# Relation sums of a graph layer: one more product of 128 columns for each tile of edges, into an unused PSUM bank

## The reference

```python
hx = jnp.einsum('ni,rio->rno', x, weight)       # 8 relations
msg = hx[edge_type, src]
agg = jax.ops.segment_sum(msg, dst, num_segments=num_nodes)
node_repr = agg * ALPHA ** 0.5 + h_bias + (x @ loop_weight) * (1.0 - ALPHA) ** 0.5
```

## Time and profile before

| | us |
|---|---|
| time, median of 3 executions | 5958.03 |
| lowest and highest of them | 5939.9 and 5958.66 |
| the profiled execution, its own time | 5956.54 |
| its span, first to last instruction | 5954.5 |

### The profile page before, as it was taken

How to read it: one execution, slowest core, us unless ns; L and a number is a source line. 1 busy time by engine, 2 the same in 40 slices (tenths; PEclk the granted TensorE clock), 3 DMA queues, 4 the chain that set the end, 5 groups by cost and what they waited for, 6 DMA issues and landing times. The chain is left out here.

```text
span 5954.5 us, 72809 instructions
## 1 busy us (share of the span) xinstructions
PE 4261.1 (72%) x18192; PEld 3031.8 (51%) x18193; DVE 2596.7 (44%) x8576; ACT 1703.5 (29%) x3913; POOL 3354.3 (56%) x3387
## 2 busy tenths in 40 slices
PE   5888877655554455557777777776768889889798
PEld 2455545423333333445555555554346667667566
DVE  7655423433343332433333333336944444444682
ACT  3343430000000000123333333333565534433330
POOL 5777665666676666245555555551456666666221
PEclk9999997766667776568787878887889999999898
DMA  6444442433333333132222222226154444444101
GB/s 218 155 157 155 159 161 84 128 92 93 93 90 91 93 95 96 28 69 41 41 43 42 41 41 41 45 39 197 39 147 141 141 119 122 120 119 120 38 1 44
DMA packets 329593, 562.66 MB, mean 94 GB/s; under 512 B 74513, under 2 KB 230302, under 8 KB 322939
## 3 DMA queue, kind: packets, MB, share of 16 engines
q0 software_dynamic: 140096, 319.55, 20.2%
q1 hardware_dynamic: 189213, 239.87, 12.8%
HBM read 459.66 MB, written 99.50 MB: 94 GB/s over the span
## 5 line engine op out<-in xcount | busy, mean ns | idle before, releaser
L963 POOL DMA_INDIRECT e_ring<-table,erow x1040 | 998.0, 960 | 516.7 <-issue 248.5
L1272 PE MATMUL e_sums<-e_ring,e_onehot 128*128 128x257 f32 x2080 | 776.5, 520 | 624.7 <-issue 312.7
L2286 POOL DMA_INDIRECT t_source<-source_rows,t_index x816 | 772.3, 946 | 709.3 <-DVE t_parts L2369 477.7
L1383 POOL DMA_INDIRECT e_ring<-table,esrc x800 | 796.1, 995 | 423.6 <-issue 207.9
L1272 PEld LDWEIGHTS e_sums<-e_ring,e_onehot 128*128 128x128 f32 x2080 | 491.2, 256 | 895.8 <-issue 535.7
L553 POOL DMA_INDIRECT r_ring<-rows,esrc x528 | 584.6, 1107 | 240.2 <-issue 133.4
L2447 PE MATMUL t_out<-t_w,t_hidden 128*128 128x256 f32 x1600 | 540.9, 474 | 169.1 <-issue 164.4
L1459 PE MATMUL e_total<-e_loads,e_times 128*128 128x256 f32 x2176 | 581.8, 400 | 38.7 <-issue 27.9
L2447 PEld LDWEIGHTS t_out<-t_w,t_hidden 128*128 128x128 f32 x1600 | 365.3, 236 | 305.6 <-issue 250.2
L1459 PEld LDWEIGHTS e_total<-e_loads,e_times 128*128 128x128 f32 x2176 | 417.6, 200 | 129.3 <-issue 55.7
L1470 PE MATMUL e_sums<-e_ring,e_onehot 128*128 128x256 f32 x1600 | 435.0, 394 | 53.7 <-DMA e_ring<-table,esrc 28.7
(11 more groups left out here) (492 smaller groups left out, 6386.5 us busy)
## 6 DMA issues: line engine op xcount, KB each, us to landing
table<-r_stage SPq DMA_DIRECT2D x49, 1024.0 KB
e_loads<-table SPq DMA_DIRECT2D x384, 128.0 KB
t_near<-near_rows SPq DMA_DIRECT2D x102, 256.0 KB
m_outputs<-first_outputs SPq DMA_DIRECT2D x49, 512.0 KB
first_outputs<-t_stage SPq DMA_DIRECT2D x96, 256.0 KB
e_ring<-table,erow POOLq DMA_INDIRECT x1040
t_source<-source_rows,t_index POOLq DMA_INDIRECT x816
e_ring<-table,esrc POOLq DMA_INDIRECT x800
```

The costliest lines, as they stand in the source:

```text
L963: eng.indirect_dma_start(ring[:, t % BODY, 0:D], None, table, bass.IndirectOffsetOnAxis(ap=b.erow[:, EARLY + t:EARLY + t + 1], axis=0)).th ...
L1272: eng.matmul(sums[g % SUMS][:, 0:ACCW], onehot[t % ONEHOTS][:, :], ring[:, t % BODY, :], start=(t % GROUP == 0), stop=(t % GROUP == GROUP ...
L1383: eng.indirect_dma_start(ring[:, t % BODY, :], None, table, bass.IndirectOffsetOnAxis(ap=b.esrc[:, FROM + t:FROM + t + 1], axis=0)).then_i ...
L2286: eng.indirect_dma_start(source[s][:, q, :], None, a.source_rows, bass.IndirectOffsetOnAxis(ap=index[s][:, q:q + 1], axis=0)).then_inc(gat ...
```

## The change

From tile 105 on, TensorE makes one more product ahead of each tile's own: the same stationary one-hot matrix with the first 128 of the slot's columns, into `turning`, started and stopped by itself. Nothing waits for it, it counts no semaphore, and nothing reads its result. It stands behind the same two waits as the tile's own product, so it starts when that one would have started, and the tile's own comes after it.

```diff
+    IDLE = P
...
                 eng.wait_ge(matched, t + 1)
                 eng.wait_ge(gathered[t % BODY], 16 * (t // BODY + 1))
+                if t > PUT(CHUNKS * PUTS):
+                    eng.matmul(turning[:, 0:IDLE], onehot[t % ONEHOTS][:, :], ring[:, t % BODY, 0:IDLE],
+                               start=True, stop=True)
                 eng.matmul(sums[g % SUMS][:, 0:ACCW], onehot[t % ONEHOTS][:, :], ring[:, t % BODY, :],
                            start=(t % GROUP == 0), stop=(t % GROUP == GROUP - 1)).then_inc(summed, 1)
```

## The result

The changed kernel took 5967.0 us (median of 20 runs), the kernel before 5948.6 us in the same set (20 runs): a ratio of 1.0036, interval 1.0023 to 1.0048. The forecast of 5845 us, faster, was wrong in sign; the time lies in the range of rival 1 (5940 to 5976), but its mechanism is another: the clock rose and did not pay for the product, as the experiments show.

What follows compares the result with a forecast made beforehand. GpSimd's gather pace was taken as the stage's floor, with late TensorE counts causing stalls; 935 gathers x (1.433 - 1.31) us gain 115 us, so 5958 - 115 = 5843, rounded to 5845 us; range 5785 to 6000.

Steps and rivals of the forecast that it cites:

- rival 1: Changed stage: late counts stay, the higher clock pays for the product; 5958 us, between 5940 and 5976; chance 0.17.
- 171 us: Gathers from 1064 to 2404 us: time lost to stalls beyond GpSimd's undisturbed pace, the most the change can win.
- its prices: Added product on TensorE: 0.25 us a tile at 2.4 GHz, 0.42 us at 1.2 GHz.
- the disputed term: TensorE's late counts in the stage shrink when it is busier: 1.31 instead of 1.433 us a gather, gaining 115 us.
- Both stretches: Before tile 105 and from 1696 to 1745 us: counts taken as prompt, so bad only where TensorE has little to do.
- the interrupted stretch: 1696 to 1745 us, gathers interrupted by seven bias pieces: counts prompt, TensorE never dry, 1.36 us a gather.
- The clock: TensorE's clock in the changed stage: rises from 0.69 to over 0.85, towards 0.95 to 0.97.
- Rival 3: TensorE in the changed stage: clock does not rise, mean 0.69, bursts grow; +140 us, 6100 us; chance 0.08.
- rival 2: At `add`: counts stay late, clock rises, bursts of eight tiles grow; +93 us, 6050 us; chance 0.17.

Runs made afterwards that it cites:

- before_again: The kernel before, unchanged, traced once more on a chip whose counts come promptly; 5056 us.
- after_again: The changed kernel once more, on the same chip as before_again; 1.0003 times the kernel before.
- set 3: Runs on a prompt chip with TensorE's counts made late through SyncE, among them relay4 and relay4_product; the kernel before took 5063 us there.
- relay4: Kernel before with one count per eight tiles, passed on by SyncE after four small transfers from group 14 on; 5300 us, 1.0469 times before.
- relay4_product: relay4 with the added product of 128 columns; 5415 us, 1.0691 times the kernel before, 115 us more than relay4.
- relay2: relay4 with two transfers instead of four, on a late chip; 6154 us, 1.0249 times the kernel before.
- relay2_product: relay2 with the added product, on a late chip; 6223 us, 1.0368 times the kernel before.
- relay_half: relay4 with its four transfers in every other six groups only, on a late chip; 6098 us, 1.0167 times the kernel before.
- relay_half_product: relay_half with the added product, on a late chip; 6126 us, 1.0203 times the kernel before.
- pause_8: Kernel before with an operation of about 1 us on GpSimd ahead of every eighth gather from the first changed tile on; 1.0174 times before.

## Why the prediction was wrong

**What held.** GpSimd's gather pace is the floor of the stage, and 171 us are what stalls take: on the prompt chips the 1040 gathers span 1317 us instead of 1514, 197 us less. The product does lie between gathers where TensorE follows them (ratios of 1.0000 to 1.0007). 1870 more matmuls ran (18192 to 20062). Of its prices the one at half clock was right and the one at full clock too high: in bursts a tile takes 0.66 us with it and took 0.48 without at the full clock, 1.29 and 0.85 at the half, so 0.18 and 0.44 instead of 0.25 and 0.42.

**The step that failed** is "the disputed term": "the counts are bad just where TensorE has little to do. I take that they shrink". They hardly did: 6.21 us late on average after 6.41, GpSimd idle 467 us instead of the forecast's 337, `add` waiting 872 us instead of well below 843. And the premise is refuted. On the prompt chips TensorE runs the same products in the same loop, at a clock of 0.61, and every count comes at once. The lateness goes with the chip on which the kernel runs.

Both stretches that were to bear the premise out were misread. Before tile 105 the counts were not prompt. GpSimd stood there for them, as the same 106 gathers show, in before from 890 to 1064 us and in before_again from 815 to 948 us:

```profile
L963 POOL DMA_INDIRECT e_ring<-table,erow x106 | 100.7, 950 | 73.7 <-PE e_sums L1272 37.3 <-issue 24.0 <-remote 12.4
```

```profile
L963 POOL DMA_INDIRECT e_ring<-table,erow x106 | 102.1, 964 | 32.3 <-issue 20.7 <-PE e_sums L1272 11.6
```

The first 104 of them came one in 1.65 us on the late chip and one in 1.27 us on the prompt one. `add` waits next to nothing there on either (1.3 and 1.2 us), because VectorE itself comes to it late, so its waits can't tell whether counts are prompt. And the interrupted stretch holds four of the seven bias pieces and not seven; the first three lie before it, and between the first and the second a count is 14.8 us late and VectorE stands for it:

```profile
1666.92 2.01 DVE L1189 TENSOR_TENSOR features<-features,e_bias 128x1792 f32<-128x1792 f32 x1
1683.81 0.48 DVE L1168 SCALAR_TENSOR_TENSOR big<-e_sums,within,big 128x257 f32 x1 [14.00 <-remote]
1685.38 2.02 DVE L1189 TENSOR_TENSOR features<-features,e_bias 128x1792 f32<-128x1792 f32 x1
```

So the pieces do not make counts prompt either. Whether a slower pace of the gathers does is not settled by any run.

**The clock** was forecast over 0.85 and reached 0.77, and TensorE's busy time was 880 us and not about 735. The direction of the clock was right. It stayed under 0.85 in the traces in which TensorE stands again and again, and where TensorE only waits for the next gather (0.98) the time didn't depend on it. Rival 3 is out: the clock rose. The page of the Trainium skill that spoke for it (TensorE: Matmul & The Clock Gate, psum-queue depth-cycling) tells of another kernel, in bf16 with 512 columns. Here the trace doesn't agree with it: in after_again every product changes bank, and the clock is 0.98.

**The size of rival 2.** Its place and its mechanism are what set 3 shows: `add` waits for TensorE, and the product makes that longer. Its price was mis-sized. I charged eight tiles at the full clock in 70 bursts, 140 us less a third. It is three tiles, mostly at the half clock, about 1.05 us behind a dry add. How that comes to so little in the change itself can be added up, since from one group's end to the next there are just three times: the count's lateness, the `add` (0.88 us), and from there to the next group's end. The sums over 115 groups (from the end of group 14 to that of group 129), in us:

```
                      whole stretch   lateness   add   to the next group's end
before                       1308.0      739.2   101.2   467.5
changed                      1333.9      707.4   101.3   525.2
relay4                       1386.8      873.3   101.3   412.2
relay4_product               1495.1      860.1   101.3   533.7
relay2                       1466.4      980.0   101.3   385.1
relay2_product               1536.3      960.5   101.3   474.4
relay_half                   1423.1      883.3   101.3   438.6
relay_half_product           1439.6      799.1   101.3   539.2
```

On the late chips the product costs 58, 89 and 101 us on the way to the next group's end, and the lateness falls by 32, 20 and 84 us. So the lateness does fall, as was forecast, but by less than the product costs; a part of that may be only that the group's last product ends later. The first pair gives 58 - 32 = +26 us for the stage. Each row is a single trace, so this is an account of these executions and not a proof; relay4 against relay4_product is what shows the mechanism, and the 28 us of relay_half_product agree with it.

**What stays open.** Why the counts of TensorE are late on some chips. Shown: on the late chips and not on the two prompt ones; TensorE's counts and not VectorE's; whoever waits, with one count in one or in eight tiles; hardly shortened by a busier TensorE; longer where there is more slack. Not tried on a late chip: pauses on GpSimd (`pause_8` fell on a prompt one), a product of another width, and a loop in which TensorE is made to stand shortly and often. One rival stands untested, the recording itself. The trace also notes each time that a semaphore counts. On the prompt chips almost no such note is missing, on the late ones many are: from tile 100 on, the trace before has 388 notes for the 947 one-hot matrices that VectorE counted, before_again 946 for 946. So on a late chip the recording loses notes, and no execution here is known to have run without it. Whether the counts of TensorE would be late without it, no run tells. No kernel here is faster than the kernel before on either kind of chip.

## What to carry to other kernels

Before costing what a change does to a stall, ask whether the stall belongs to the kernel: a count that arrives 10 us after its engine went idle need not be so on the next chip, and a run of the kernel before on another chip would have told that. Work added to an engine with half its time idle is free only while it follows a steady producer; behind each standstill it is exposed in the few items that the next wait needs, and there, in these traces, the engine ran at its lower clock. A higher granted clock was worth nothing where nobody waited for a matmul (0.61 to 0.98, ratio 1.0003). And a short wait on a count doesn't show that the count was prompt: the one who waits may have come late himself.

## What the runs showed of the hardware

- The same kernel took 5056 to 5063 us on two chips and 5949 to 5999 us on the others, up to 19% more. The loops with gathers take the difference: from the first to the last gather 822, 1514, 1473 and 1220 us for L553, L963, L2286 and L1383 in the first trace, 746, 1317, 1029 and 1050 us in before_again. A gather of L963 itself takes the same, 0.96 us, on both. A part of the difference may come from the recording (above).
- On late chips a count of TensorE can be seen up to 17.5 us after the end of its product by SyncE, with one count for eight tiles, while others of the same stretch are seen at once (relay2). VectorE's counts reach TensorE within 0.1 us on the same chips.
- Behind standstills of 11.94 us (changed kernel) and 6.30 us (relay4_product) TensorE's first tiles ran at 1.2 GHz, as the rows of both show, though work was there (1.29 us a tile with the added product, against 0.66 us a few tiles later).
- Added products of one, 128 and 256 columns in each tile went with a granted clock of 0.56, 0.98 and 0.99 on a prompt chip, against 0.61 without one; none of them changed the time.
